# Expert tables of one byte a word, loaded eight words at a time

## What is computed

```
# first layer: 8 experts, hidden 512, the best 2 of 8 a token
probs = softmax(xf @ Wr + br);  vals, idx = top_k(probs, 2)
out += cw_e * (relu(xf @ W1_e + b1_e) @ W2_e + b2_e)     # over all experts e
# second layer: 8 groups of 8 experts, hidden 256,
# the best 2 groups, the best 2 experts in each: 4 of 64 a token
h = relu(xt @ W1[g, e] + b1[g, e]);  y = h @ W2[g, e] + b2[g, e]
```

## Time and profile before

| what | us |
|---|---|
| median of 3 runs | 1134.4 |
| the profiled execution, first to last instruction | 1221.9 |
| its first expert loop | about 257 to 388 |
| its second expert loop | about 795 to 1142 |

### The profile page before, as it was taken

The page is one execution under the profiler, slowest core; times in us unless marked ns, Lnnn a source line. Parts: engine busy times, 40 slices in busy tenths (PEclk is TensorE's granted clock), DMA queues, the critical chain, the costliest instruction groups (busy, mean ns, idle before and its releaser), DMA issues.

```text
span 1221.9 us, 18019 instructions
## 1 busy us (share of the span) xinstructions
PE 802.4 (66%) x5133; PEld 637.8 (52%) x5133; DVE 778.2 (64%) x2305; ACT 437.9 (36%) x1233; POOL 510.6 (42%) x528
## 2 busy tenths in 40 slices
PE   0218963879998248778587511287887897888343
PEld 0105552679998124434255401177776787777332
DVE  7885467656665248888766699855555555666642
ACT  2543241524444134443103304533343444444200
POOL 7841001255540634662101002466664435555574
PEclk9759965579999556666665555599999998999755
DMA  2290089012221287566400404133332223333222
GB/s 69 76 403 37 1 249 309 1 50 70 71 66 38 60 143 140 118 143 131 77 1 1 132 0 127 33 85 85 89 83 81 83 77 87 88 96 94 59 72 75
DMA packets 116599, 112.95 MB, mean 92 GB/s; under 512 B 16403, under 2 KB 102994, under 8 KB 116258
## 3 DMA queue, kind: packets, MB, share of 16 engines
q1 hardware_dynamic: 103228, 84.68, 25.3%
q0 software_dynamic: 13280, 27.13, 8.2%
HBM read 76.15 MB, written 35.57 MB: 91 GB/s over the span
## 4 chain that ended last, share of the span: by engine, by line
PE 55%; DVE 22%; issue 9%; POOL 5%; ACT 4%; DMA 3%; another core or an unknown queue 1%; SPq 0%; DVEq 0%; POOLq 0%; ACTq 0%
PE ps L638 18%; PE ps L645 15%; DVE wide L1348 6%; PE ps L1969 4%; POOL wide L810 3%; PE ps L633 3%; DVE wide L1229 3%; PE ps L2231 3%; PE ps L2139 2%; PE ps L2180 2%; ACT wide L1757 2%; DVE bnst L955 2%; POOL wide L874 1%; PE ps L2076 1%; PE ps L2224 1%
## 5 line engine op out<-in xcount | busy, mean ns | idle before, releaser
L645 PE MATMUL ps<-big,wide 128*128 x1568 | 238.1, 282 | 33.9 <-ACT wide L605 20.6
L638 PE MATMUL ps<-wide 128*128 (+1 forms) x1580 | 247.1, 287 | 18.9 <-DVE wide L554 12.2
L867 POOL DMA_INDIRECT wide<-xrows,holder x189 | 182.8, 967 | 158.1 <-PE ps L633 116.1
L559 DVE TENSOR_SCALAR wide<-ps,wide 128x128 f32<-128x128 f32 x395 | 131.7, 348 | 156.9 <-PE ps L638 138.4
L638 PEld LDWEIGHTS ps<-wide 128*128 128x128 f32 x1580 | 206.2, 195 | 40.8 <-issue 32.9
L645 PEld LDWEIGHTS ps<-big,wide 128*128 128x128 f32 x1568 | 203.7, 194 | 44.5 <-issue 43.9
L605 ACT ACTIVATE wide<-ps,wide 128x128 f32<-128x128 f32 x395 | 137.8, 367 | 202.4 <-PE ps L638 184.9
L1348 DVE TENSOR_REDUCE wide<-ps 125x3 f32<-125x1500 f32 (+1 forms) x96 | 143.7, 1540 | 46.7 <-PE ps L1969 45.3
L874 POOL DMA_INDIRECT wide<-results,place x128 | 127.6, 997 | 100.1 <-DVE h L1328 44.0
L1969 PE MATMUL ps<-big 97*125 97x500 bf16 x256 | 104.8, 545 | 40.3 <-DVE wide L1348 32.5
L623 ACT COPY wide<-ps 128x128 f32<-128x128 f32 x322 | 85.2, 264 | 92.1 <-PE ps L645 78.1
(11 more groups left out here) (388 smaller groups left out, 1102.7 us busy)
## 6 DMA issues: line engine op xcount, KB each, us to landing
results<-wide SPq DMA_DIRECT2D x161, 128.0 KB, 1.8
big<-kappa SPq DMA_DIRECT2D x8, 1750.0 KB, 21.0
big<-parts SPq DMA_DIRECT2D x96, 125.0 KB
big<-in_L_ffn_W_dram SPq DMA_DIRECT2D x10, 1024.0 KB, 9.4
big<-in_L_ffn_W_dram SPq DMA_DIRECT2D x64, 128.0 KB, 2.6
parts<-wide SPq DMA_DIRECT2D x24, 250.0 KB
xrows<-wide SPq DMA_DIRECT2D x2, 1792.0 KB
wide<-results,place POOLq DMA_INDIRECT x192
```

Of the source, the lines that this page charges most:

```text
L559: last = v.tensor_scalar(ring.hid[u % 2][:, 128 * k:128 * k + 128], ps[:, 4 + u % 2, 128 * k:128 * k + 128], w[:, hid + k:hid + k + 1], 0. ...
L638: last = t.matmul(ps[:, (2 if k < c.HC // 2 else 4) + u % 2, 128 * k:128 * k + 128], ring.w1[u % U][:, 128 * k:128 * k + 128], turned, sta ...
L645: last = t.matmul(ps[:, 6 + u % 2, 0:D], ring.hid[u % 2][:, 128 * k:128 * k + 128], w[:, D * k:D * k + D], start=k == 0, stop=k == c.HC - 1)
L867: gp.indirect_dma_start(ring.rows[j % RING], None, xrows[:, :], bass.IndirectOffsetOnAxis(ap=holder[:, j:j + 1], axis=0)).then_inc(S(f"row ...
```

## The change

The tables are now bytes: the expert's number and the block's place in the ring, without their factors. `value` multiplies by the factor in the address arithmetic. `Words.load` takes a count. TensorE loads 16 words at the start and 8 (four tiles) behind every fourth tile, VectorE loads one word a tile: 8 at the start, and 8 at the top of each round of eight tiles. Two operations less write the tables of a layer.

```
-        table = sb("table", [1, 2 * TAB], I32)
+        table = sb("table", [1, 4 * TAB], U8)
...
-                for u in range(0, RING, 2):
-                    self.load(0, u)
...
-            def load(self, first_tile, u):
-                self.engine.reg_load(self.regs[2 * u:2 * u + 4], self.table[0:1, bass.ds((first_tile + (self.first + u)) * 2, 4)])
+            def load(self, row, at_, count, first=0):
+                self.engine.reg_load(self.regs[first:first + count], row[0:1, at_:at_ + count])
+
+            def value(self, n, which, scale):
+                word = self.engine.snap(self.regs[n], min_val=0, max_val=max(self.tops))
+                word = nc.s_assert_within(word, 0, self.tops[which], skip_runtime_bounds_check_because="the tables hold clipped numbers")
+                return word * scale
...
-            w1, _ = pairs_of(mybir.EngineType.DVE, stage_tables[c.n], 0, 2, (c.E - 1) * c.wcols, (KEEP[c.n] - 1) * 128)
-            words = Words(dve, p, stage_tables[c.n], 2, (c.E - 1) * c.wcols, (KEEP[c.n] - 1) * 128)
+            words = Words(dve, p, RING, (c.E - 1, KEEP[c.n] - 1))
+            words.load(tile_tables[c.n], 0, RING)
...
             def tiles(first_tile, count):
+                words.load(stage_tables[c.n], first_tile, count)
                 for u in range(count):
...
-                    stage(words.value(u, 0), u + 3)
-                    if u % 2 and first_tile + u + RING < c.tiles:
-                        words.load(first_tile + RING, u - 1)
+                    stage(words.value(u, 0, c.wcols), u + 3)
...
-            words = Words(pe, p, tile_tables[c.n], 0, (c.E - 1) * c.HC * D, (KEEP[c.n] - 1) * 128)
+            words = Words(pe, p, 2 * RING, (c.E - 1, KEEP[c.n] - 1))
+            words.load(tile_tables[c.n], 0, 2 * RING)
...
-                    second(words.value(u, 0), u)
-                    if u % 2 and first_tile + u + RING < c.tiles:
-                        words.load(first_tile + RING, u - 1)
+                    second(words.value(2 * u, 0, c.HC * D), u)
+                    if u % 4 == 3 and first_tile + u + RING - 3 < c.tiles:
+                        words.load(tile_tables[c.n], 2 * (first_tile + RING + u - 3), 8, 2 * u - 6)
...
-                me.did(TS(tiles_[:, :, 0], one, float(c.HC * D), None, ALU.mult))
-                me.did(TS(stages_[:, 0:tab - 1, 0], one[:, 1:tab], float(c.wcols), None, ALU.mult))
-                me.then(TS(wrap, numbers, float(keep), -128.0 * keep, ALU.is_ge, ALU.mult))
-                me.did(v.scalar_tensor_tensor(stages_[:, :, 1], numbers, 128.0, wrap, ALU.mult, ALU.add))
+                me.did(v.tensor_copy(tiles_[:, :, 0], one))
+                me.did(v.tensor_copy(stage_tables[f][:, 0:tab - 3], one[:, 3:tab]))
                 me.settle()
-                me.then(TS(wrap, block, float(keep), -128.0 * keep, ALU.is_ge, ALU.mult))
-                me.then(v.scalar_tensor_tensor(tiles_[:, 0:tab - 1, 1], block[:, 1:tab], 128.0, wrap[:, 1:tab], ALU.mult, ALU.add))
+                me.then(TS(wrap, block, keep, -keep, ALU.is_ge, ALU.mult))
+                me.then(TT(out=tiles_[:, 0:tab - 1, 1], in0=block[:, 1:tab], in1=wrap[:, 1:tab], op=ALU.add))
```

More of the change, by code:

```diff
@@ L21 @@
 U32 = mybir.dt.uint32
+U8 = mybir.dt.uint8
 ALU = mybir.AluOpType
@@ L261, in tower_kernel @@
         b1r = sb("b1r", [128, 2, 128])
-        table = sb("table", [1, 2 * TAB], I32)
+        table = sb("table", [1, 4 * TAB], U8)
         w0 = 2 * FFN[0].tab
-        assert 2 * w0 <= 2 * TAB <= 512
-        tile_tables = [table[0:1, 0:w0], cst[0:1, 128:128 + 2 * TAB].bitcast(I32)]
-        stage_tables = [table[0:1, w0:2 * w0], table[0:1, 0:2 * TAB]]
+        assert w0 % 16 == 0 and w0 + FFN[0].tab <= TAB
+        tile_tables = [table[0:1, 0:w0], table[0:1, TAB:3 * TAB]]
+        stage_tables = [table[0:1, w0:w0 + FFN[0].tab], table[0:1, 3 * TAB:4 * TAB]]
         place = [sb("place", [128, 4, NT], I32)] * 2
@@ L457, in weight_loads, with __init__ @@
             return c.E // (8 if c.n else 4) + (W2_EARLY if c.n else 8)
[L459 to L467, removed]
-        class Words:
-            def __init__(self, engine, p, table, first, top_a, top_b):
-                self.engine, self.table, self.first, self.tops = engine, table, first, (top_a, top_b)
-                self.regs = [engine.alloc_register(f"{p}word{n}") for n in range(2 * RING)]
-                for u in range(0, RING, 2):
-                    self.load(0, u)
-            def load(self, first_tile, u):
-                self.engine.reg_load(self.regs[2 * u:2 * u + 4], self.table[0:1, bass.ds((first_tile + (self.first + u)) * 2, 4)])
-            def value(self, u, which):
-                word = self.engine.snap(self.regs[2 * u + which], min_val=0, max_val=max(self.tops))
-                return nc.s_assert_within(word, 0, self.tops[which], skip_runtime_bounds_check_because="the tables hold clipped numbers")
+        class Words:
+            def __init__(self, engine, p, count, tops):
+                self.engine, self.tops = engine, tops
+                self.regs = [engine.alloc_register(f"{p}word{n}") for n in range(count)]
+            def load(self, row, at_, count, first=0):
[4 more added lines that the diff above has]
+                return word * scale
             def free(self):
@@ L571, in expert_vector @@
             v.tensor_copy(ring.blocks[:, 0:128], ps[:, 0, 0:128]).then_inc(S(p + "blocks_in"), 1)
-            stage(w1[0], 1)
+            stage(words.value(2, 0, c.wcols), 1)
             dve.wait_ge(S(p + "turned"), 2)
             v.tensor_copy(ring.blocks[:, 128:256], ps[:, 1, 0:128]).then_inc(S(p + "blocks_in"), 1)
-            stage(w1[1], 2)
+            stage(words.value(4, 0, c.wcols), 2)
             dve.wait_ge(S(p + "hid_filled"), 3)
@@ L1152, in route @@
                 dve.wait_ge(S("emptied_dve"), nth[at[f"expert{f}", 0]])
-                keep = KEEP[f]
+                keep = float(KEEP[f])
                 numbers = tileno[0:1, 0:tab]
-                tiles_, stages_ = (t_.rearrange("o (t w) -> o t w", w=2) for t_ in (tile_tables[f], stage_tables[f]))
+                tiles_ = tile_tables[f].rearrange("o (t w) -> o t w", w=2)
+                me.did(TT(out=block, in0=numbers, in1=one, op=ALU.subtract))
                 if f:
-                    me.did(TT(out=block, in0=numbers, in1=one, op=ALU.subtract))
                     me.then(TS(second, one, float(c.E), None, ALU.is_ge))
```

4 lines of the change are left out of this document (1 added, 3 removed).

## The result

| | median us | runs | spread |
|---|---|---|---|
| before | 1135.2 | 4 | 1134.3 to 1139.8 |
| changed | 1282.8 | 4 | 1276.0 to 1292.2 |

The ratio is 1.129, its 95% interval 1.123 to 1.134. The forecast was 1123 us, the range 1112 to 1138: wrong in sign and far outside, and outside of all three rivals too.

A forecast was written before the change was run, and what follows sets the result against it. Neither TensorE nor VectorE was taken as the bound throughout; table loads were thought to hold up TensorE in the second loop. Terms -5.2 - 3.2 - 1.1 - 1.5 + 0.4 - 1.0 = -11.6 us: 1134.4 to 1122.8, range 1112 to 1138.

The forecast's parts named there:

- What a load of eight costs: Register loads of eight bytes: taken as one round trip to the table, 0.33 us, the same as four words.
- rival 2: Table loads pay by the word, 0.61 us for eight; 1137 us, slightly slower; chance 0.13.
- Rival 3: Table loads: a byte costs as much as the worst word, 0.14 us, 1.18 for eight; 1167 us; chance 0.10.
- The loads fall in number, so their cost falls: TensorE's second loop: 26 late and 16 middle loads fewer at 0.20 us, gaining 5.2 and 3.2 us.
- What a load shows with: Time a four-word load costs TensorE in the second loop: taken as 0.20 us, between 0.09 and 0.40.
- The balance: Second loop less the trace's 87.5 us surplus, less 238 us of passes: 21.5 us over 126 loads, 0.17 each.
- First loop covered, 0: First expert loop: all of TensorE's loads are hidden beside its work, so the change gains 0 there.
- VectorE's loads, 0: One load of eight at the top of each round is covered by VectorE's copy: 0, bound 3 us.
- The early part, 0, for GpSimd's sake: Second loop up to tile 77: 19 loads fewer, but GpSimd's gathers set the pace: 0, bound 3.8 us.
- Starts: Starts of the loops: fewer loads on the chain gain 1.5 us in the second loop, 1.1 in the first.
- Arithmetic: Addresses: one more multiplication each, some 5 ns, counting behind 42 TensorE loads: +0.4 us, upper bound 2.1.
- The table writing: Writing the tables, on the chain: two operations go, gaining 1.0 us.

The follow-up runs named there:

- e_words_8: The changed kernel with table elements of four-byte words instead of bytes, same loads in the same places: 1140.1 us, 1.001 of the kernel before.
- e_words_premultiplied: The changed kernel's order of loads, but four-byte words holding the products, so no added multiplication in the addresses: 1137.4 us, 1.001 of the kernel before.
- the undisturbed trace: Second trace of the kernel before, nothing changed: span 1136.2 us, median 1138.6 us; the trace behind the prediction had a span of 1221.9 us.

## Why the prediction was wrong

- **What a load of eight costs** is the step that failed. "One round trip" (0.33 us) was argued from the narrow spread of 126 lengths, which shows only that loads of one shape are alike. Words in whole groups of four cost 0.07 to 0.08 us each, as rival 2 had it (0.61; measured 0.59 to 0.64). Bytes cost 0.24 to 0.27 each, so the load that was to take 0.33 us takes 2.19, and TensorE stands 2.26 us behind every fourth tile. Rival 3 named the right mechanism, a byte as dear as a bad word, but took its price, 0.14, from a delayed load of words; no row of before had a narrow element, and a bound from below and above by rows of words didn't bound it.
- The Trainium skill, "Runtime: NRT & Kernel Launch", section "Instruction fetch mechanics", with its 200 ns a register, would have given 1.6 us and +65 us. That is nearer than any of my cases, and its form was right: for narrow elements the trace shows 240 to 270 ns each, while for eight or sixteen aligned words it is 70 to 80. I set it aside because a row of words contradicted its size.
- **The loads fall in number, so their cost falls** (26 and 16 loads fewer, 8.4 us) failed even for words: what counts is the sum of words loaded, which the change leaves as it was. e_words_8 and e_words_premultiplied show 0 where 11.6 us were forecast.
- **What a load shows with** was mis-sized: 0.32 us late in the undisturbed trace, not 0.20. The balance gave all 87.5 us to the second loop; it held 68.3, so 21 us too little were left in it for the loads. The trace's own 0.40 was nearer than the balance.
- **First loop covered, 0**: true for loads up to 0.6 us (134.2 to 135.5 us in every such run), false for 1.92 us, which is what a load of eight bytes takes there: +18.6 us. A cover has a size, and none was written beside the 0.
- **VectorE's loads, 0**: false by 18 us at 2.1 us a load when they stand alone; at 0.6, in e_words_8, its trace has no stall ahead of `second` in the late part.
- **The early part, 0, for GpSimd's sake**: right for loads taken away. With the bubbles gone the early part is 94 us as before, and only the middle and late parts gain. Loads of 2.2 us GpSimd doesn't hide: the early part of the changed kernel is 129 us.
- **Starts**: with words the way from the last step ahead of the loop to `first` is 0.3 to 0.4 us shorter in both loops, which is the prediction's other case ("shrink to 0.4 us each"), not its 1.5 and 1.1. With bytes TensorE's load of sixteen leads the chain. The chain of the changed kernel at the second loop has these rows (start, length, what):

```profile
795.46 0.22 DVE holder L1203
795.68 4.13 issue
```

- **Arithmetic**: 10 ns for an operation more on TensorE (49/53/59 to 58/63/68) and 12 on VectorE (55 to 67), not 5. Against the loads it doesn't matter. The table writing (-1.0 us) can't be told from the spread of the stretch between the loops.
- **Not foreseen at all**: with the pauses of 2.2 us TensorE's clock falls. By the trace the second loop's 134.5 us are these two. Over all weight loads of the loop, what their distances have beyond the 0.11 us of a pass grew by 97 us in the pauses and by 38 us in the stretches at the lower clock, together 135. The first part stands below as idle time behind "issue", which goes from 15 to 124 us; that is more than 97 because this view leaves out the short gaps of the kernel before.

The waits of the weight-load queue within the second loop, of the changed kernel and of the kernel before:

```profile
PEld ps L622 <- issue: 65.8, 35, 2.0
...
PEld ps L627 <- issue: 58.0, 38, 2.2
```
```profile
PEld ps L638 <- issue: 15.4, 69, 0.3
```

## What to carry to other kernels

A load of registers from a table pays for each element, and only words in whole groups of four are cheap: keep the elements words of four bytes, their number a multiple of four and every load's start at a multiple of 16 bytes, and don't save bytes there. Before fewer or larger loads, look for the place where the sequencer waits anyway, and keep each load shorter than that wait: the place brought 1.7%, the merging nothing. And before a balance is drawn between a trace and the runs, take a second trace: one execution can be a bad one.

## What the runs showed of the hardware

- A register load of words that starts at a multiple of 16 bytes: 0.33 us for 4, 0.59 to 0.64 for 8, 1.10 for 16, but 0.53 for 2 and 0.82 for 6. Of one or two bytes an element, or of words starting 4, 8 or 12 bytes off (4 and 12 on VectorE alone): 0.52 for 2 (bytes), 0.95 for 4, 1.83 to 2.19 for 8, 3.97 to 4.00 for 16. TensorE's and VectorE's sequencers agree where both were seen.
- With idle stretches of 2.2 us every four tiles TensorE's mean granted clock is 0.87 to 0.92, where it was 0.98 to 1.00 without them; with the same bytes loaded in pieces of 0.52 us, and half of the idle time gone, it stays at 0.98 to 1.00. The Trainium skill, "TensorE: Matmul & The Clock Gate", section "Part 1: The HAM clock gate (the "warmup" mystery)", describes a gate that lets half of the pulses through when the engine has been idle; the doubled distance of the passes (0.86 against 0.44 us) agrees.
- A shift to the right within an address instruction makes it 79 ns long where it was 49 (a multiplication more: 58); a mask wasn't fused and cost two instructions of 29 and 32 ns.
